# A graph-attention kernel on one core: half of each chunk's rank picks on ScalarE, compares with immediates, and a last stage without a scaling pass

## The reference

```python
h = jnp.maximum(_layernorm(x, axis=-1), 0.0)
edge_h = jnp.concatenate([h[src], edge_attr_128], axis=1)
edge_m = jnp.einsum('ef,of->eo', edge_h, a)              # 100000 x 128
powers = -jax.nn.leaky_relu(edge_m @ a_2[0], negative_slope=0.2)
edge_e = jnp.exp(powers)
e_rowsum = segment_sum(edge_e, src)                      # 0 -> 1e-12
h_prime = segment_sum(edge_e[:, None] * edge_m, src)
return x + h_prime / e_rowsum[:, None]
```

## Time and profile before

| | |
|---|---|
| median of 3 runs | 1217.61 us (1216.38 to 1219.86) |
| span of the profiled execution, first to last instruction | 1750.0 us |
| VectorE (DVE) busy in it | 927.9 us |
| POOL busy in it | 761.5 us |
| TensorE (PE) busy in it, mean granted clock | 724.3 us, 0.64 of 2.4 GHz |
| ScalarE (ACT) busy in it | 340.7 us |
| queues' packets | 51.6% of 16 engines' span |

### The profile page before, as it was taken

How to read it: one execution, slowest core, us unless ns; L and a number is a source line. 1 busy time by engine, 2 the same in 40 slices (tenths; PEclk the granted TensorE clock), 3 DMA queues, 4 the chain that set the end, 5 groups by cost and what they waited for, 6 DMA issues and landing times. The chain is left out here.

```text
span 1750.0 us, 21538 instructions
## 1 busy us (share of the span) xinstructions
PE 724.3 (41%) x5452; PEld 595.4 (34%) x5453; DVE 927.9 (53%) x2932; ACT 340.7 (19%) x1343; POOL 761.5 (44%) x814
## 2 busy tenths in 40 slices
PE   2610161104555016101265146565025547664977
PEld 2600040003444014000244134444024446443866
DVE  6538383335656846323344846554234467552787
ACT  4521102221121110212111111122111111120005
POOL 1055525555455351565555253455555451555000
PEclk9855575556666557555566557567556557666999
DMA  9687535365673330635675153573555433414765
GB/s 343 185 304 262 178 117 181 108 215 189 193 227 103 135 95 19 193 101 181 208 248 163 47 190 97 150 259 103 183 195 166 139 110 105 142 54 169 215 240 157
DMA packets 188554, 291.72 MB, mean 167 GB/s; under 512 B 19287, under 2 KB 125878, under 8 KB 188214
## 3 DMA queue, kind: packets, MB, share of 16 engines
q1 hardware_dynamic: 143940, 162.33, 30.1%
q10 hardware_dynamic: 19442, 75.36, 12.8%
q0 software_dynamic: 25088, 53.04, 8.7%
HBM read 159.04 MB, written 131.61 MB: 166 GB/s over the span
## 5 line engine op out<-in xcount | busy, mean ns | idle before, releaser
L505 POOL DMA_INDIRECT ordered_rows<-feed,dest x784 | 754.9, 963 | 842.1 <-issue 721.6
L736 PE MATMUL psum<-back,hots 128*128 128x129 f32 x2128 | 410.5, 344 | 215.7 <-issue 183.5
L736 PEld LDWEIGHTS psum<-back,hots 128*128 128x128 f32 x2128 | 352.0, 245 | 277.3 <-issue 275.7
L976 DVE TENSOR_TENSOR chosen<-psum,window_hot 128x400 f32<-128x400 f32 x98 | 55.9, 570 | 595.5 <-remote 568.2
L708 PE MATMUL psum<-score_parts,place_hot 128*128 128x50 bf16 x2352 | 109.4, 210 | 482.2 <-DVE place_hot L957 310.2
L708 PEld LDWEIGHTS psum<-score_parts,place_hot 128*128 128x128 bf16 x2352 | 98.9, 114 | 494.7 <-DVE place_hot L957 316.5
L578 ACT ACTIVATE feed<-leaky 128x8 f32<-128x8 f32 (+1 forms) x98 | 21.2, 216 | 1230.5 <-DVE leaky L989 578.9
L586 ACT ACTIVATE feed<-feed 128x128 f32<-128x128 f32 (+1 forms) x784 | 238.6, 387 | 0.0
L966 DVE SCALAR_TENSOR_TENSOR junk<-feed,psum 128x128 bf16<-128x128 f32 x784 | 169.9, 280 | 0.0
L1037 DVE TENSOR_TENSOR hots<-psum,back 128x1024 f32<-128x1024 f32 x133 | 161.9, 1217 | 4.1 <-DMA back<-ordered_rows 4.1
L1020 DVE TENSOR_TENSOR acc<-acc,psum 128x387 f32 (+1 forms) x133 | 73.7, 554 | 104.7 <-remote 76.3
(11 more groups left out here) (143 smaller groups left out, 416.0 us busy)
## 6 DMA issues: line engine op xcount, KB each, us to landing
ordered_rows<-empty SPq DMA_DIRECT2D x19, 3696.0 KB, 21.8
back<-ordered_rows ACTq DMA_DIRECT2D x133, 528.0 KB
feed<-in_edge_attr SPq DMA_DIRECT2D x97, 512.0 KB
place_rows<-places SPq DMA_DIRECT2D x98, 256.0 KB
ordered_rows<-feed,dest POOLq DMA_INDIRECT x784
self_part<-acc ACTq DMA_DIRECT2D x1, 3234.0 KB, 11.7
feed<-self_part SPq DMA_DIRECT2D x1, 3234.0 KB
out<-feed SPq DMA_DIRECT2D x6, 448.0 KB
```

The costliest lines, as they stand in the source:

```text
L505: pool.indirect_dma_start(out=ordered, out_offset=bass.IndirectOffsetOnAxis(ap=dest[:, n:n + 1], axis=0), in_=feed[:, n * ROW:(n + 1) * RO ...
L736: last = pe.matmul(psum[:, bass.ds(outs[u], FEAT + 1)], hots[:, hot_buffer(k) * GT + u, :], back[:, n:n + FEAT + 1], start=False, stop=u = ...
```

## The change

Three edits, in one diff.

1. `count_chunk` makes `hot` with 50 `tensor_scalar` instructions, one a bucket, each comparing `bucket` (bfloat16) with an immediate number, in place of one `tensor_tensor` with broadcast operands. For chunks 1 to 4 a further VectorE instruction then multiplies the upper half (25 buckets) of `count` by `hot`, in place.
2. For chunks 1 to 4 VectorE makes picks for buckets 0 to 24 alone, into three buffers, without the wait on its own last pick. For buckets 25 to 49 the pick is split: TensorE adds the masked `count` (bfloat16) with 25 matmuls (`count_sums`), and ScalarE makes `hot * shift` in float32 into two buffers (`shift_chunk`), which TensorE adds as before. TensorE's order is: the 25 count matmuls, then one pick of VectorE and one of ScalarE in turn. ScalarE does its part where `PLAN` has the rank. Chunk 0 keeps its 50 picks.
3. The last stage works in units of three windows (17 units). TensorE transposes `acc` directly, without `inv`; ScalarE copies three transposes at once; TensorE multiplies; VectorE multiplies the product by `inv` as it adds it.

```diff
 def shift_chunk(c):                       # new, ScalarE
+                tiles = CHUNKS[c] * RT
+                act.wait_ge(hots_done, (c + 1) * BUCKETS)
+                act.wait_ge(bases_done, c + 1)
+                for j in range(DVE_HALF):
+                    b, k, n = DVE_HALF + j, DVE_BUFS + j % ACT_BUFS, (c - 1) * DVE_HALF + j
+                    if j >= ACT_BUFS:
+                        act.wait_ge(shifts_added, n - ACT_BUFS + 1)
+                    act.activation(picked[:, k * tiles:(k + 1) * tiles], hot[:, b * tiles:(b + 1) * tiles], ACT.Copy,
+                                   scale=shift[:, b:b + 1]).then_inc(shifts_done, 1)
...
+            def half_sums(c):             # TensorE; count_sums(c) ahead of it
+                for b in range(DVE_HALF):
+                    k, a = b % DVE_BUFS, DVE_BUFS + b % ACT_BUFS
+                    pe.wait_ge(picks_done, picks_before(c) + b + 1)
+                    pe.matmul(ranks(c, SUMS, tiles), ident[:, :], picked[:, k * tiles:(k + 1) * tiles], ...)
+                    pe.wait_ge(shifts_done, (c - 1) * DVE_HALF + b + 1)
+                    pe.matmul(ranks(c, SUMS, tiles), ident[:, :], picked[:, a * tiles:(a + 1) * tiles], ...)
+            def count_sums(c):
+                pe.wait_ge(counted_done, c)
+                pe.wait_ge(picks_done, picks_before(c) + 1)
+                for b in range(DVE_HALF, BUCKETS):
+                    pe.matmul(ranks(c, SUMS, tiles), ident_bf[:, :], count[:, b * tiles:(b + 1) * tiles], ...)
...
-                dve.tensor_tensor(hot[:, 0:flat].rearrange("p (b t) -> p b t", t=tiles),
-                                  bucket[:, t0:t0 + tiles].rearrange("p (a t) -> p a t", a=1).to_broadcast(shape),
-                                  numbers.rearrange("p (b a) -> p b a", a=1).to_broadcast(shape),
-                                  ALU.is_equal).then_inc(hots_done, 1)
+                for b in range(BUCKETS):
+                    dve.tensor_scalar(hot[:, b * tiles:(b + 1) * tiles], bucket[:, t0:t0 + tiles], float(b), None,
+                                      ALU.is_equal).then_inc(hots_done, 1)
...
+                if c > 0:
+                    dve.wait_ge(ends_done, c + 1)
+                    half = slice(DVE_HALF * tiles, flat)
+                    dve.tensor_tensor(count[:, half], count[:, half], hot[:, half], ALU.mult).then_inc(counted_done, 1)
...
-                    if c > 0:
-                        dve.wait_ge(picks_done, n + 1)
...
+            for n in range(FIN_UNITS):    # TensorE, last stage
+                for k, w in enumerate(range(NW * n, min(WINDOWS, NW * n + NW))):
+                    last = pe.transpose(bank(n % 2, k * P, P), acc_w[:, w, 0:FEAT], ident[:, :])
+                last.then_inc(scaledT_done, 1)
+                if n > 0:
+                    last_products(n - 1)
...
+            def result(n):                # VectorE, last stage
+                dve.wait_ge(out_ready, n + 1)
+                for k, w in enumerate(range(NW * n, min(WINDOWS, NW * n + NW))):
+                    dve.wait_ge(self_added, w + 1)
+                    dve.scalar_tensor_tensor(out=fin_x[:, w, 0:FEAT], in0=bank(2 + n % 2, k * P, P), scalar=inv[:, w:w + 1],
+                                             in1=fin_x[:, w, 0:FEAT], op0=ALU.mult, op1=ALU.add).then_inc(result_done, 1)
```

More of the change, by code:

```diff
@@ L71 @@
 BB = 5
+DVE_HALF, DVE_BUFS, ACT_BUFS = 25, 3, 2
+NW = 3
+FIN_UNITS = -(-WINDOWS // NW)
 ADD_LAG = 2
@@ L624, in _ @@
                     constants()
+                elif what == "rank" and at[0] > 0:
+                    shift_chunk(at[0])
                 elif what == "feed":
@@ L630, in _ @@
                     run_pairs(act, *at, step, feed_group)
[L633 to L642 removed]
+            for n in range(FIN_UNITS):
+                cnt = min(WINDOWS, NW * n + NW) - NW * n
+                act.wait_ge(scaledT_done, n + 1)
+                act.copy(last_T[:, n % 2, 0:cnt, :].rearrange("p k f -> p (k f)"), bank(n % 2, 0, cnt * P)).then_inc(scaledT_copied, 1)
         @block.tensor
@@ L674, in first_tiles, with pick_sums @@
                   .then_inc(first_done, 1)
-            def pick_sums(c, i):
+            def pick_sums(i):
+                tiles = CHUNKS[0] * RT
+                for k in range(BB):
+                    pe.wait_ge(picks_done, i * BB + k + 1)
+                    pe.matmul(ranks(0, SUMS, tiles), ident[:, :], picked[:, k * tiles:(k + 1) * tiles],
+                              start=i == 0 and k == 0, stop=k == BB - 1, skip_group_check=True)\
+                      .then_inc(picks_added, 1)
+            def half_sums(c):
                 tiles = CHUNKS[c] * RT
-                first = isinstance(i, int) and i == 0
-                for k in range(BB):
-                    pe.wait_ge(picks_done, c * BUCKETS + i * BB + k + 1)
+                for b in range(DVE_HALF):
+                    k, a = b % DVE_BUFS, DVE_BUFS + b % ACT_BUFS
+                    pe.wait_ge(picks_done, picks_before(c) + b + 1)
                     pe.matmul(ranks(c, SUMS, tiles), ident[:, :], picked[:, k * tiles:(k + 1) * tiles],
-                              start=first and k == 0, stop=k == BB - 1, skip_group_check=True)\
-                      .then_inc(picks_added, 1)
+                              start=False, stop=False, skip_group_check=True).then_inc(picks_added, 1)
+                    pe.wait_ge(shifts_done, (c - 1) * DVE_HALF + b + 1)
+                    pe.matmul(ranks(c, SUMS, tiles), ident[:, :], picked[:, a * tiles:(a + 1) * tiles],
+                              start=False, stop=b == DVE_HALF - 1, skip_group_check=True).then_inc(shifts_added, 1)
+            def count_sums(c):
+                tiles = CHUNKS[c] * RT
+                pe.wait_ge(counted_done, c)
+                pe.wait_ge(picks_done, picks_before(c) + 1)
+                for b in range(DVE_HALF, BUCKETS):
+                    pe.matmul(ranks(c, SUMS, tiles), ident_bf[:, :], count[:, b * tiles:(b + 1) * tiles],
+                              start=b == DVE_HALF, stop=False, skip_group_check=True)
             def table_sums(c):
@@ L782, in _, with last_products @@
             pe.wait_ge(acc_done, STEPS)
-            def last_products(i):
-                for k in range(RG):
-                    pe.wait_ge(scaled_done, RG * i + k + 1)
-                    if not isinstance(i, int) or i > 0:
-                        pe.wait_ge(result_done, RG * (i - 1) + k + 1)
-                    pe.transpose(bank(k, 0, P), stage[:, k, :], ident[:, :]).then_inc(scaledT_done, 1)
-                for k in range(RG):
-                    pe.wait_ge(scaledT_copied, RG * i + k + 1)
-                    pe.matmul(bank(k, P, P), stageT[:, k, :], A2T[:, :], start=True, stop=True).then_inc(out_ready, 1)
-            last_products(0)
-            with pe.Fori(1, WINDOWS // RG) as i:
-                last_products(i)
+            def last_products(n):
+                pe.wait_ge(scaledT_copied, n + 1)
+                if n >= 2:
+                    pe.wait_ge(result_done, NW * (n - 1))
+                for k in range(min(WINDOWS, NW * n + NW) - NW * n):
+                    last = pe.matmul(bank(2 + n % 2, k * P, P), last_T[:, n % 2, k, :], A2T[:, :], start=True, stop=True)
+                last.then_inc(out_ready, 1)
+            for n in range(FIN_UNITS):
+                if n >= 2:
+                    pe.wait_ge(scaledT_copied, n - 1)
+                for k, w in enumerate(range(NW * n, min(WINDOWS, NW * n + NW))):
[3 more added lines that the diff above has]
+                    last_products(n - 1)
+            last_products(FIN_UNITS - 1)
         @block.vector
```

70 lines of the change are left out of this document (30 added, 40 removed).

## The result

The kernel after takes **1214.24 us** (median of 20 runs, 1211.22 to 1216.90); the kernel before, beside it, 1216.32 (20 runs, 1213.68 to 1219.86). The ratio is 0.9981, 95% interval 0.9973 to 0.9990: 2.3 us less, and between 1.2 and 3.3. The forecast was 7.8 us less. The direction and the range held; over two thirds of the gain is not there. The forecast started from 1217.61, the median of three runs; the median of twenty is 1.3 us lower. The profiled execution is the fastest of the 20, 1211.22 us, so its parts sum to less than the median.

What follows compares the result with a forecast made beforehand. With POOL's scatters a close candidate, it took VectorE's sorts to show in the time: start -0.9, counts -3.2, ranks -4.8, last stage +1.1, sum -7.8, 1217.6 to 1209.8 us; range 1204 to 1214, 8 in 10 within 1202 to 1222.

Steps and rivals of the forecast that it cites:

- What bounds the kernel: Whole kernel: POOL's scatters or VectorE's order binds once the trace's 532 us of waits are gone; sorts' savings taken to show.
- rival (a): Sorts: POOL's queue hides them, only start and end count, +0.2 us, 1217.8; chance 0.30.
- The sorts' savings show, in full or nearly: Counts and ranks of chunks 1 to 4: their shorter times reach the kernel's time; chance 0.44.
- the 100 us that were left over in that sum: Of 1217.6 us, some 100 left for the last chunk's 14 pair steps and times POOL has nothing to scatter.
- Ranks: Ranks of chunks 1 to 4: picks shared out, TensorE becomes the bound; -1.9, -1.9, -3.8 and +2.8, sum -4.8 us.
- Counts: Counts of chunks 1 to 4: faster masks less the new multiplication, -3.2 us; bounds +14 and -7.
- The start: Chunk 0's masks, ahead of the first scatter: 5.0 for 5.9 us, -0.9, +0.6 at most.
- The last stage: Last stage: VectorE at 0.524 us a window, 24.6 to 25.7 us, +1.1.
- Rival (b), the stopped descriptors,: Chunks 1 to 4: no scatter advances during the small compares, +23.3 + 0.2 us, 1241; chance 0.07.
- Rival (d): Ranks: TensorE has the same float32 picks, so nothing gained in any rank; -3 us, 1214.6; chance 0.09.

Runs made afterwards that it cites:

- e1_before: The kernel before, unchanged, run again for a trace that is not stretched by foreign waits: 1216.25 us, ratio 1.0002.
- e2_end_only: The kernel before with the new last stage alone: 1216.51 us, ratio 1.0003 to the kernel before.
- e14_before_plans: The kernel before with only PLAN changed, more groups fed ahead of chunk 1's sort and chunk 4's sort one round earlier: 1197.49 us.
- e3_old_end: The kernel after with the last stage of the kernel before: 1215.37 us, ratio 0.9994 to the kernel before.
- e6_more_plain: The kernel after with the old mask instruction run ahead of the new masks in chunks 2 to 4: 1217.99 us, ratio 1.0020 to the kernel before.

## Why the prediction missed

**What bounds the kernel.** This is the step that failed, and it failed where the text chose. It had both candidates, POOL's 784 scatters at 1.26 us and VectorE's order, and named the right first one; then it let the 34.85 us of POOL's idleness after the rank of chunk 2 decide against rival (a), gave "The sorts' savings show, in full or nearly" 0.44, and put the whole -3.2 and -4.8 into its sum. That row came from a span with 532 us of waits that the runs don't have, as the text itself says two paragraphs earlier; `e1_before` shows no such wait. The mechanism of rival (a) was the true one for chunks 2 and 3, with the bound that the text gave it: "between sorts VectorE paces a fed group in less than half of POOL's 10.1 us". Of the 100 us that were left over in that sum 26 are POOL's waits at chunk 1, 11 stops, and some 61 lie between the last scatter and the last stage. This last part was the second thing missing: the text never asked which sort lies behind POOL's last gate and is paid whatever the queue holds, and that is chunk 4's.

**The sorts, one by one.** From the first mask to the CAST of the ranks, with the groups fed between them, before (`e1_before`) and after: chunk 1 82.0 and 76.8, chunk 2 86.2 and 81.6, chunk 3 64.6 and 59.5, chunk 4 39.3 and 41.8 us. That is -12.4 for a forecast of -8.0, and it comes in three parts.

- Ranks, from the first pick to the CAST: 25.9 to 23.8, 25.6 to 24.2, 22.4 to 18.8 and 22.1 to 23.3, in all -5.9, for forecasts of -1.9, -1.9, -3.8 and +2.8, in all -4.8. TensorE is the bound in chunks 1, 2 and 4, as said (busy for 23.0 of 23.7 us in chunk 1), and VectorE waits 41.5 us for it. The clock stood at 0.50 for the whole rank of chunk 4.
- Counts, from the first mask to the end of the product, or of the small copy behind the scan before: 35.5 to 34.0, 35.5 to 33.9, 26.8 to 26.7 and 9.3 to 11.7, in all -0.8 for -3.2. The term was mis-sized: the masks of 224 and 168 tiles took 0.5 to 0.6 us more than priced, the products 0.1 to 0.2.
- Between the two, where nothing was priced, -5.7. Before, VectorE stood behind a count until TensorE had looked up the next group. The product fills that wait, so it costs the sort 1.4 us less than its own length:

```profile
427.21 0.21 DVE L839 COPY ends<-count 128x50 bf16<-128x50 bf16 x1
428.82 0.57 DVE L976 TENSOR_TENSOR chosen<-psum,window_hot 128x400 f32<-128x400 f32 x1 [1.40 <-PE psum L708]
```

These are from `e1_before`, chunk 2, and the other three have the same 1.40. After, the same instruction follows the products of chunks 1 to 3 without a wait, and waits 0.48 us in chunk 4. What each sort is worth to the kernel is another matter: chunk 1's shows as 4 us of POOL's waits, those of chunks 2 and 3 (-9.7) not at all, and chunk 4's +2.5 in full.

**The start** (-0.9). The count is 1.0 us shorter (4.86 for 5.87). The first scatter comes at 93.5 on average in the fourteen traces with the new masks in chunk 0 and at 94.4 in the three with the old (`e1_before`, `e2_end_only`, `e14_before_plans`): -0.9, as forecast. Single ones go from 92.0 to 94.8, so three traces can't tell this well, and in the one profile of after it is only -0.2, because the rank of chunk 0 behind it gives up to 1 us back.

**The last stage** (+1.1). In the profiles it is 32.4 for 31.7; in runs +0.4 (-0.9 to +1.7). Right in sign and size as far as this can be told.

**Rival (b), the stopped descriptors,** got 0.07. Its mechanism is real and its price was too high: 23.3 us if no scatter moved in any compare. Measured in chunks 2 to 4, the compares stopped one scatter for 0.7 us in the profile of after and for 3.6 to 5.3 in six others. The product, which the prediction did not suspect at all, stops one in nearly every sort; with it the long stops there are 4.5 us in the profile of after and 7.5 to 9.4 in five others with the same instructions. And the row that the prediction missed for (b), "a scatter lengthened beside L957", was in its own rows: the scatter at 701.14 us of the earlier trace rows takes 1.10 us, and this is VectorE beside it in the same trace.

```profile
700.92 0.49 DVE L957 TENSOR_SCALAR place_hot<-place_rows,lane 128x1024 bf16 x1
```

The scatter starts 0.22 us into it and ends 0.83 us after it, as the others do. Over all 784 scatters such a stop is lost in the mean, 0.963 for 0.96, and each is at most 0.24 us because the instruction is short. So "The trace doesn't bear the rule out at that size" rested on the mean of a row where single scatters would have shown the stop.

**The sum, made again** for the profiled executions: first scatter -0.2, waits -4.0, stops -2.8, sort 4 +2.5, end +0.7, together -3.8 of the -5.0 between the spans of `e1_before` and after; where the other 1.2 us lie is not shown. The stops of that one execution were few. In `e3_old_end` and `e6_more_plain`, with the same small compares and products, they are 7 to 9 us more, 4.0 of which, at the masks of chunk 1, only shorten the wait behind them. That would put a typical run 3 to 5 us over the profiled one; the median is 3.0 over it.

**What was luck.** That the time fell at all hangs on small terms of both signs, of which the stops were not in the forecast's sum. Rival (d) named 1214.6, nearest to the 1214.24 measured, by another mechanism: nothing gained in any rank, where three ranks gained 1.4 to 3.6 us that the kernel doesn't show. Rival (a) had the mechanism for chunks 2 and 3, and its +0.2 is nearer to the measured -2.3 than the forecast's -7.8.

## What to carry to other kernels

Price an edit where it stands on the path: with a queue eight groups deep in front of the engine that binds, a microsecond saved or lost in a sort was worth about one where the queue ran empty (chunk 1), about one behind the last point at which the queue gates (chunk 4), and nothing between them. Look for those two places in an undisturbed trace before pricing anything, and distrust an idle row from a span that is much longer than the runs. When POOL issues indirect DMAs all the time, keep a vector instruction from reading two operands in SBUF beside it: with one of them in PSUM the same 11.8 us instruction cost no scatter anything. And look at single scatters, not at their mean.

## What the runs showed of the hardware

- A scatter (an indirect DMA issued by POOL, 0.96 us) stands while VectorE runs an instruction with two tensors in SBUF, and ends 0.83 us after it: 11.70 us beside 11.82, 6.55 beside 5.99, 3.28 beside 3.08; with one operand in PSUM it takes 0.96 beside 11.8. Of several products of 3.07 us in a row each stopped one scatter.
- `place_hot`, a `tensor_scalar` of 1024 bf16 numbers and 0.48 us, stops a scatter in the same way. In the traces of the kernel after and of the sixteen runs 330 scatters started at least 0.11 us after its start and 0.15 us before its end, and all of them ended 0.82 to 0.84 us after its end.
- Small compares with an immediate, of 224 numbers and one every 0.13 us, can stop a scatter until 0.12 us after the last of the row, for 0.7 to 5.3 us beyond its 0.96 in the 50 of chunk 2. Nineteen of the 40 that started 0.05 to 0.08 us into a compare were stopped, and none that started elsewhere in one. With VectorE waiting for its own end after each no scatter took over 1.21 us, at 0.16 us more a compare. Why one is stopped and another not is open.
- Without stops the scatters pace at 1.265 us, and no two starts were less than 1.25 us apart in any of these traces.
- The product of two plain 2-byte operands takes 0.55 ns an element (3.08 us for 5600), `scalar_tensor_tensor` on the same data 1.07.
